# Graph attention kernel: edge lists and node inputs made in one stage, the rest of the lists beside the relation maxima, node maxima split during their gathers

## The reference

```python
h = relu(layernorm(x))
# first layer, for each relation r:
xr = (h @ W_rel[r]).reshape(N, H, D)
es, ed = einsum('nhd,hd->nh', xr, a_s[r]), einsum('nhd,hd->nh', xr, a_d[r])
logit = where(mask, leaky_relu(es[src] + ed[dst], 0.2), -1e30)
mx = segment_max(logit, dst)                    # one value per node, relation and head
p = exp(logit - mx[dst]) * mask
out = segment_sum(p / segment_sum(p, dst)[dst] * xr[src], dst)
# then gelu, W_cross, a softmax over relations; second layer: edge messages, segment_sum, two node products
```

## Time and profile before

| | us |
|---|---|
| median of 3 runs (5531.38 to 5540.8) | 5537.8 |
| profiled run | 5538.13 |
| its span | 5536.3 |
| lists, to the issue of node_inputs' first load | 239.2 |
| node_inputs, to the first gather of relation_maxima | 376.7 |
| relation_maxima, to the first operation of node_maxima | 1442.9 |
| node_maxima, to the first load of the attention | 1549.1 |

### The profile page before, as it was taken

How to read it: one execution, slowest core, us unless ns; L and a number is a source line. 1 busy time by engine, 2 the same in 40 slices (tenths; PEclk the granted TensorE clock), 3 DMA queues, 4 the chain that set the end, 5 groups by cost and what they waited for, 6 DMA issues and landing times. The chain is left out here.

```text
span 5536.3 us, 106419 instructions
## 1 busy us (share of the span) xinstructions
PE 3325.0 (60%) x16923; PEld 2273.1 (41%) x16924; DVE 3895.1 (70%) x11905; ACT 1426.1 (26%) x2966; POOL 3890.5 (70%) x3803
## 2 busy tenths in 40 slices
PE   0062222222156676244687877877887878778868
PEld 0031111111046665233354554545555545455537
DVE  4635555555578888887587777777777777777765
ACT  0130000000056666433322222222222222222222
POOL 3127777777679999721378888888878787888870
PEclk9685555555567778577899999999999999999989
DMA  2266666666256666412688888888888888888874
GB/s 57 60 182 194 193 196 192 194 194 193 81 126 153 154 155 154 150 42 76 183 183 182 179 180 179 180 179 179 178 177 182 177 180 177 180 179 182 177 144 141
DMA packets 725012, 891.72 MB, mean 161 GB/s; under 512 B 123241, under 2 KB 555465, under 8 KB 724710
## 3 DMA queue, kind: packets, MB, share of 16 engines
q0 software_dynamic: 217200, 396.10, 35.3%
q1 hardware_dynamic: 450742, 392.89, 24.9%
q10 hardware_dynamic: 56976, 101.87, 6.0%
HBM read 652.36 MB, written 238.06 MB: 161 GB/s over the span
## 5 line engine op out<-in xcount | busy, mean ns | idle before, releaser
L1529 POOL DMA_INDIRECT sums<-msg_bsum,k_sidx x831 | 1323.0, 1592 | 285.5 <-issue 241.7
L731 POOL DMA_INDIRECT max_xe<-rows,l_index x832 | 800.6, 962 | 426.6 <-issue 253.3
L1543 POOL DMA_INDIRECT msg_ga<-ab,k_bsrc x832 | 828.4, 996 | 368.7 <-issue 200.1
L1631 ACT ACTIVATE msg_low_ps<-msg_xs 128x512 f32<-128x512 f32 x928 | 558.0, 601 | 1986.8 <-DVE msg_xs L1600 1971.6
L1666 PEld LDWEIGHTS msg_both_ps<-msg_onehot,msg_hid 128*128 128x128 f32 x3712 | 552.0, 206 | 1216.7 <-DVE msg_bsum L1573 688.0
L1679 PE MATMUL msg_pre_ps<-msg_rw,msg_lt 128*128 128x512 f32 x1856 | 1030.0, 638 | 8.9 <-DMA msg_rw<-ab 8.9
L1666 PE MATMUL msg_both_ps<-msg_onehot,msg_hid 128*128 128x64 f32 x3712 | 616.4, 292 | 511.6 <-DVE msg_bsum L1573 500.4
L942 POOL TENSOR_SCALAR att_keyhot<-k_ramp,att_keys 128x128 f32<-128x128 f32 x1028 | 702.0, 703 | 56.1 <-ACT att_keys L1014 54.5
L1610 DVE TENSOR_TENSOR msg_hid<-msg_xs,msg_low_ps 128x512 f32<-128x512 f32 x928 | 634.5, 684 | 88.4 <-ACT msg_low_ps L1631 69.9
L1668 PE MATMUL msg_both_ps<-msg_hid,msg_same 128*128 128x256 f32 x1856 | 654.3, 437 | 0.0
L1599 DVE TENSOR_TENSOR msg_xs<-msg_pre_ps,msg_ga 128x256 f32<-128x256 f32 x928 | 388.9, 419 | 362.4 <-issue 157.4
(11 more groups left out here) (292 smaller groups left out, 5351.3 us busy)
## 6 DMA issues: line engine op xcount, KB each, us to landing
msg_rw<-ab SPq DMA_DIRECT2D x928, 128.0 KB
l_outside<-xe SPq DMA_DIRECT2D x1028, 72.0 KB, 2.7
xe<-max_xe SPq DMA_DIRECT2D x104, 576.0 KB, 3.0
max_src<-srcs ACTq DMA_DIRECT2D x104, 512.0 KB, 3.8
att_keyrow<-key ACTq DMA_DIRECT2D x257, 128.0 KB, 3.5
msg_lt<-in_efT SPq DMA_DIRECT2D x928, 32.0 KB
rows<-node_rows SPq DMA_DIRECT2D x50, 288.0 KB, 2.4
max_begin<-begin ACTq DMA_DIRECT2D x104, 128.0 KB, 2.5
```

The source lines that it names most:

```text
L731: pool.indirect_dma_start(xe[:, b, u, :], None, T.rows, bass.IndirectOffsetOnAxis(ap=K.index[:, k:k + 1], axis=0)).then_inc(s_xe[b], 16)
L1529: pool.indirect_dma_start(T.sums[k % 2], bass.IndirectOffsetOnAxis(ap=K.sidx[:, k:k + 1], axis=0), bsum[:, (k + 1) % SB, :], None, compute ...
L1543: pool.indirect_dma_start(ga[:, (k + 1) % RB, :], None, T.ab, bass.IndirectOffsetOnAxis(ap=K.bsrc[:, k:k + 1], axis=0)).then_inc(s_ga[k % ...
L1631: act.activation(low_ps[u % 2][:, :], xs[:, u % 2, :], ACT.Copy, scale=SLOPE1).then_inc(s_low, 1)
```

## The change

The stage `lists` goes. A phase `list` holds what outlives a stage (thresholds, gathered destinations, semaphores), and two stages share its work. `node_inputs` does the two counts of the windows at its start, the `rec` fields after x has been centred, and one count and one gather for each node tile inside the tile loop; six moves lie on ACT and PE before the loop, the last four of them between root and first normalisation. `relation_maxima` runs the rest on DVE in ticks 2 to 27 of its 104 (`beside`), with the first 32 ticks unrolled; the 17 gathers of steps, the keys, their moves and stores come after the group loop. `node_maxima` splits the `ed` term and then each half of the gathered maxima as soon as it is there, in separate buffers, with half of the copies on ACT.

```diff
-def lists(nc, K, T):
...
+def node_inputs(nc, K, T, S):
...
         @block.sync
         def _(sp):
+            sp.dma_start(first[:, :], T.first.to_broadcast([P, BLOCKS])).then_inc(s_first, 16)
             sp.dma_start(x[:, :, :], T.x.rearrange("(t p) c -> p t c", p=P)).then_inc(s_x, 16)
...
             sp.dma_start(att[:, :], T.att).then_inc(s_w, 16)
+            sp.dma_start(rec[:, :, :], T.rec[0:NB * P, :].rearrange("(j e) f -> j e f", e=GE)).then_inc(s_rec, 16)
...
+        @block.gpsimd
+        def _(pool):
...
+            for t in range(TILES):
+                c = t + 2
+                pool.wait_ge(S.s_made, INDEX + t + 1)
+                settle(pool, K)
+                pool.indirect_dma_start(S.dst[:, c, :], None, T.dst,
+                                        bass.IndirectOffsetOnAxis(ap=S.block_i[:, c:c + 1], axis=0)).then_inc(S.s_get, 16)
...
+            def count(t, b):
+                if past(t, 2):
+                    dve.wait_ge(s_cnt, t - 1)
+                dve.tensor_scalar(junk[:, b, :], first[:, :], S.thr[:, ds(t + 2, 1)], 0.0, ALU.is_lt, ALU.add,
+                                  accum_out=blocks[:, ds(t + 2, 1)]).then_inc(s_cnt, 1)
+
+            def number(t, b):
+                dve.wait_ge(s_cnt, t + 1)
+                dve.tensor_scalar(S.block_i[:, ds(t + 2, 1)], blocks[:, ds(t + 2, 1)], 1.0, 0.0,
+                                  ALU.subtract, ALU.max).then_inc(S.s_made, 1)
+
-            pipeline(dve, TILES, 2, [(0, evacuate), (1, rest)])
+            pipeline(dve, TILES, 2, [(0, evacuate), (0, count), (1, rest), (1, number)])
...
 def relation_maxima(nc, K, T, S):
...
+            pool.wait_ge(S.s_made, STEPLIST)
+            settle(pool, K)
+            for k in range(KKC):
+                pool.indirect_dma_start(kstep[:, k, :, :].rearrange("p f e -> p (f e)"), None, T.blk,
+                                        bass.IndirectOffsetOnAxis(ap=kplan.b[:, k:k + 1], axis=0)).then_inc(s_kget, 16)
+            for k in range(KC):
+                pool.indirect_dma_start(step[:, k, :, :].rearrange("p f e -> p (f e)"), None, T.blk,
+                                        bass.IndirectOffsetOnAxis(ap=plan.b[:, k:k + 1], axis=0)).then_inc(s_sget, 16)
...
+            def beside(t):
+                if t == 2:
+                    boundaries()
+                elif t == 4:
+                    offsets()
+                elif t == 5:
+                    kplan.pairs(dve, L, K, off[:, 0:KWINDOWS + 1], K.kgrid[:, :])
+                elif t == 8:
+                    plan.pairs(dve, L, K, off64[:, :], K.grid[:, :])
+                elif t == 10:
+                    schedule()
+                elif 12 <= t < 17:
+                    position(2 + (t - 12) * 10, 2 + (t - 11) * 10)
+                elif t == 17:
+                    lasts()
+                elif 18 <= t < 28:
+                    present((t - 18) * 5, (t - 17) * 5)
...
-            pipeline(dve, GROUPS, RG, [(2, scan), (1, separate), (2, firsts)])
+            ticks(dve, GROUPS, RG, 2, tick, AHEAD)
             dve.wait_ge(s_dup, 4 * GROUPS)
+            dve.wait_ge(s_kget, 16 * KKC)
...
 def node_maxima(nc, K, T, acc):
...
+            def split(g, values):
+                s, k = parts[g]
+                for i in range(TERMS):
+                    part = term[:, s, i, k, :]
+                    ins = dve.tensor_copy(part, values[:, k, :])
+                    if i < TERMS - 1:
+                        L.link(ins)
+                        L.link(dve.tensor_tensor(values[:, k, :], values[:, k, :], part, ALU.subtract))
+                    else:
+                        ins.then_inc(s_term, 1)
+                dve.wait_ge(s_term, g + 1)
+                for i in range(TERMS):
+                    for q in range(KQ // 2):
+                        for r in range(R):
+                            out, src = to_keys(s, i, k, q, r)
+                            dve.tensor_copy(out, src).then_inc(s_keyed, 1)
...
+            split(0, rest)
             L.mark(dve.memset(acc[:, :, :], 0.0))
-            dve.wait_ge(s_run, 16 * TILES)
...
+            for g in range(1, len(parts)):
+                s, k = parts[g]
+                n = k.stop - k.start
+                dve.wait_ge(s_run[g - 1], 16 * n)
```

More of the change, by code:

```diff
@@ L44 @@
 REC = 6
+THR = 2 + TILES
 PAD_DST = 1 << 20
@@ L303, in lists, with move_waits @@
+AT_NODES = INDEX + TILES
+DIAG, STEPLIST, KEY, LOC = range(AT_NODES + 1, AT_NODES + 5)
+def move_waits(pe, S, kind, row):
+    if kind == "row":
+        pe.wait_ge(row, 3)
+    elif kind == "index":
+        pe.wait_ge(S.s_made, INDEX)
+    elif kind == "key":
+        pe.wait_ge(S.s_made, KEY)
+    elif kind == "src":
+        pe.wait_ge(row, 16 * KC)
+    else:
+        pe.wait_ge(S.s_made, LOC)
+def node_inputs(nc, K, T, S):
+    with Phase(nc, "node") as ph:
         NG = NB // G
         GE = G * P
-        THR = 2 + TILES
@@ new lines, in node_inputs @@
+        tp_ps = [ph.ps(f"tp_ps{b}", [P, 4, P]) for b in range(2)]
+        s_first, s_rec, s_row, s_cnt = (ph.sem(n) for n in ("first", "rec", "row", "cnt"))
+        by_group = lambda t: t[:, :].rearrange("e (j u) -> e u j", u=G)
+        moves = []
+        for u in range(0, G, 4):
+            moves.append(("index", [index[:, v * P:(v + 1) * P] for v in range(u, u + 4)], by_group(K.index)[:, u:u + 4, :]))
+        for u in range(0, G, 4):
+            moves.append(("row", [fields[:, v, 0, :] for v in range(u, u + 4)], by_group(K.bsrc)[:, u:u + 4, :]))
@@ new lines, in node_inputs @@
+        for u in range(0, G, 4):
+            moves.append(("row", [fields[:, v, 2, :] for v in range(u, u + 4)], by_group(typT)[:, u:u + 4, :]))
+        NA = 2 * R + 2
+        RH = R * H
+        YS = 2 * RH
+        YW = YS + C + 2 * H
+        x = ph.sb("x", [P, TILES, C])
+        squares = ph.sb("squares", [P, TILES, C])
+        mean = ph.sb("mean", [P, TILES])
+        rstd = ph.sb("rstd", [P, TILES])
+        w_rel = ph.sb("w_rel", [P, R, C])
+        w_y = ph.sb("w_y", [P, YW])
+        w_t = ph.sb("w_t", [P, R + 1, C])
@@ new lines, in relation_maxima @@
+def relation_maxima(nc, K, T, S):
+    with Phase(nc, "max") as ph:
+        GROUPS = NB // G
+        RG = 4
+        RH = R * H
+        AHEAD = 32
+        xe = ph.sb("xe", [P, RG, G, XW])
+        begin = ph.sb("begin", [RH, 2, G * P])
+        m = ph.sb("m", [P, 2, G, RH])
+        run = ph.sb("run", [RH, 2, G * P])
+        runT = ph.sb("runT", [P, RG, G, RH])
+        srcf = ph.sb("srcf", [P, NB])
+        real = ph.sb("real", [P, 1])
+        src = ph.sb("src", [P, 2, G, P])
+        junk = ph.sb("junk", [P, G, P], BF16)
+        dup = ph.sb("dup", [P, G])
+        rowf = ph.sb("rowf", [P, G])
+        mT_ps = [ph.ps(f"mT_ps{b}", [RH, G * P]) for b in range(2)]
+        runT_ps = [ph.ps(f"runT_ps{b}", [P, G, RH]) for b in range(2)]
+        tile = ph.sb("tile", [P, P])
+        thr0 = ph.sb("thr0", [P, TILES])
@@ L804, in _ @@
             pipeline(act, GROUPS, RG, [(3, move_back), (1, begins), (1, sources)])
+            for g, (kind, ins, out) in enumerate(moves):
+                act.wait_ge(S.s_tp, MOVED + g + 1)
+                act.activation(out, tp_ps[g % 2][:, 0:len(ins), :], ACT.Copy).then_inc(S.s_cp, 1)
         @block.tensor
@@ L824, in back, with tick @@
                 last.then_inc(s_bk, 1)
-            pipeline(pe, GROUPS, RG, [(2, back), (1, transpose)])
+            def tick(t, h, has):
+                if isinstance(t, int) and t == 3:
+                    pe.wait_ge(S.s_made, DIAG)
+                    pe.matmul(off_ps, K.ones[:, :], flat(diag[:, :, :]), start=True, stop=True).then_inc(S.s_off, 1)
+                if has(2):
+                    back(t - 2, (h - 2) % RG)
+                if has(1):
+                    transpose(t - 1, (h - 1) % RG)
@@ L829, in node_maxima @@
+            ticks(pe, GROUPS, RG, 2, tick)
+            for g, (kind, ins, out) in enumerate(moves):
+                move_waits(pe, S, kind, s_sget)
+                if g >= 2:
+                    pe.wait_ge(S.s_cp, MOVED + g - 1)
+                for u, a in enumerate(ins):
+                    last = pe.transpose(tp_ps[g % 2][:, u, :], a, K.ident[:, :])
+                last.then_inc(S.s_tp, 1)
 def node_maxima(nc, K, T, acc):
     with Phase(nc, "top") as ph:
-        CH = 10
-        S2 = 2 * H
```

660 lines of the change are left out of this document (298 added, 362 removed).

## The result

The changed kernel takes 5338.75 us (median of four runs, 5335.70 to 5342.85) where the kernel before takes 5537.61: a ratio of 0.964, 95% interval 0.9627 to 0.9654. The forecast was 5348 with a range of 5315 to 5392, and the result lies in it. The profiled run took 5335.7, its span is 5333.8, against 5538.1 and 5536.3, so the two traces differ by 202.5 us in their spans.

| stretch | before | after | difference | forecast |
|---|---|---|---|---|
| to the first gather of the maxima | 376.7 | 165.7 | -211.0 | -204.3 |
| relation maxima | 1066.2 | 1093.8 | +27.7 | +29.9 |
| node maxima | 106.2 | 88.5 | -17.7 | -15.9 |
| all the rest | 3987.2 | 3985.7 | -1.5 | 0 |

What follows compares the result with a forecast made beforehand. No resource full in `lists`, a serial DVE-POOL-DVE chain; POOL's gathers set relation maxima. Terms -204.3 + 17.9 + 12 - 25.9 + 10 = -190.3 from 5538.1 gave 5348 us, range 5315 to 5392.

Steps and rivals of the forecast that it cites:

- Stage 1: Start to first gather of the maxima: 376.7 us falls to 172.4, a change of -204.3.
- The tile: Loop of node_inputs: 2.15 us a tile over the present 1.8, bounds 1.8 and 3.13, adding 17.5 us over 50 tiles.
- Rival A: Tile loop keeps its pace, the stores' turn absorbing the counts: -17.5, total 5330 us; chance 0.15.
- The tail: After the tile loop: four `outside` ops and the last gather's landing instead of a store's, +1.2 us.
- Stage 2: Relation maxima: DVE's added work hidden, 17 step gathers behind the 832 cost +17.9, slowed gathers +12 us.
- 0.69: Relation and node maxima: POOL loses 0.69 us per us of long two-input or wide DVE work; +12 and +10 us.
- Stage 3: Node maxima: split work overlapped with gathers ends the stage earlier, -25.9 us, less +10 for gathers slowed by DVE.
- rival C: Relation and node maxima: DVE and POOL exclude each other in full, +20 and +12 us, total 5381; chance 0.15.
- D: Tile loop: the added work comes serially, 3.13 us a tile, +49, total 5397 us; chance 0.12.
- E: Tile loop can't start until the counts are through: +56, total 5404 us; chance 0.03.
- F: Tile loop: gather and count hold each other up, stores queue behind; slower than before, 5538 us and more; chance 0.02.
- B: Relation and node maxima: long DVE operations cost POOL's gathers nothing, -22, total 5326 us; chance 0.08.

Runs made afterwards that it cites:

- second trace: The changed kernel itself run again, unedited, on chip 2 beside later variants: 5339.05 us, ratio 0.9641 to the kernel before.
- the pair of kernels with 2560 elements: Changed kernel plus one long unused DVE sum over 128 x 2560 elements per maxima group, on two operands or on one: 5630.2 and 5424.6 us.

## Why the prediction was right, and where its steps were off

**Stage 1, up to the tile loop: right.** Vectors landed at 23.67 (22.5 forecast), the sums began at 45.21 (45.5), the first normalisation at 55.96 (57.2). That `rec` queues behind x on SP cost about what was put down: DVE's cast of it began at 38.00. One thing was missed, and it was small: that cast took 2.81 us where it had taken 1.08, beside a cast of POOL's on the same data.

**The tile: inside its bounds, the reason wrong.** 2.15 was taken, between 1.8 and 3.13, and 1.914 came: 0.12 a tile were added and not 0.35. The step "it comes to 2.08, over the 1.8 at which two buffers of stores now turn" added the new work to a busy time. DVE's real sum is 1.73 a tile, and by the kernels with the counts first and the gathers behind even that isn't what counts: the loop with all the counts and no gathers is as quick as before. By the waits the bound was the stores all along. The step that failed is that the added engine work was priced, and POOL's gather, which was said not to be the bound, was only brought in by its bytes to confirm it. Rival A (the counts are absorbed in the wait for the stores) was right on its own ground; what it left out was the gather. Against the forecast this gave 50 x 0.236 = 11.8 us, some 10 by the second trace.

**The tail: 1.2 forecast, 6.3 more came.** This is the step that was most wrong for its size. From the last gather's end to the first act of the next stage it is 7.3 us, and to POOL's first gather there 7.9. With the counts first, where gathers had been done for 85 us, DVE's last operation ended at 206.15 and the next stage began at 206.65, 2.8 us after the issue of the last store. With all gathers behind the loop DVE was done at 149.65, the last gather ended at 211.47, and the next stage began 7.3 us later, at 218.74. So it is the gather that the border follows, and not DVE's work. Without the comparisons nothing was gained (7.9 us), and without POOL's wait for the landing 5.7 us were left. A border right behind a gather costs some 3 to 5 us more than one behind stores; POOL's wait for the landing is some 1.6 of it, and what the rest is stays open. -1.2 (the first normalisation) - 11.8 + 6.3 makes the -6.7 by which stage 1 beat its forecast; the 6.3 is what the other two leave.

**Stage 2: right in its sum.** The 832 gathers grew by 8.7 us (8 forecast), and from the last of them to the next stage it is 31.2 us in place of 12.2, +19.0 (17.9 and 4). That two-operand work holds a gather for 0.7 of its time is shown by the pair of kernels with 2560 elements. But of the 8.7 us it is only 4.4. Another 6.7 are spread evenly: the median gather takes 955 ns after and 947 before, 8 ns x 832, and all kernels with the changed lists have 955 or 958, on all chips. The short counts held gathers for some 2 us less than before, which makes up the sum; in the second trace of the changed kernel they held them for 1 us more, and the growth is 12.4 us. What lengthens each by 8 ns wasn't found. So this term came out right by luck, with half its cause wrong: 0.69 had been charged on 11 us, and DVE had some 9 us of two-operand work there. That the 68 us of DVE's work would be hidden was right (392.5 us of waits for a gather are left).

**Stage 3: right, two errors against each other.** The gathers took 5.5 us more (10 forecast): seven of them were held, three beside the first split and four beside that of the first half, and the 22.7 us of clearing beside them held none. The copies on ACT took 0.39 us and not 0.28; the stated bounds were 0.15 and 0.38 "each", the upper one being the row for 256 elements, and the row was right although the copy is of 200 elements in 32 partitions. It cost 2.6 us. What the prediction's own sums have wrong is small: the split adds up to 3.8 and not 3.9, and rival C to 5380 and not 5381.

**The rivals.** C, D, E and F fell by the total, and C by the 0.70 too: the lock is held in full, but the gather under way when DVE begins isn't stopped. B (long operations of DVE cost POOL nothing) fell by the pair of kernels. A was half right, as said. What no rival foresaw is the one effect that could have spoilt the forecast: the 308 instructions (526 with waits and accumulator reads) that DVE gained ahead of its loop of the messages. By luck they ended where nothing is fetched again; 12 more, and the changed kernel would have come out at 5429, with every step of the argument as it was.

## What to carry to other kernels

Before you add work to a loop, ask what ends its waits. This loop waited for its stores: DVE's counts beside it cost nothing, up to 0.96 busy, and a further gather on POOL cost 0.12 us a turn or more. Work laid beside POOL's gathers is sorted by its form: a long operation on two tensors stops POOL for 0.7 of its time, and a reduction or a comparison that counts into an accumulator does the same work free; a plain comparison with a scalar or a cast may stop it too, so look at the gather beside it. And when a stage that no edit touches changes length, compare the packets of fetched instructions and how many instructions stand ahead of the loop, waits included, before anything else.

## What the runs showed of the hardware that was not expected

- A loop of DVE instructions (260, or 315 with waits) is fetched again in each turn, or not, by where it stands: 12 instructions moved the kernel from 88 to 363 packets and by 89.8 us on chip 2; two kernels lost some 200 on chip 0.
- Chips differ in one stage above all: the gathers of the maxima are served at 156 GB/s on chip 0 and at 192 or 193 on the others, while the messages of the kernels with 83 to 89 packets take 2659 to 2669 us on chip 0 and 2647 to 2655 on the others.
- Which operations hold POOL's indirect gathers: sums, products and comparisons of two f32 tensors (the next gather ends 0.83 us behind a sum over 2560 elements), four comparisons of one f32 tensor with a scalar and casts from f32 to bf16 (0.11 and 0.12 us behind); hardly a reduction (2.81 us), and not counts with an accumulator (1.07 us) or a clearing (22.7 us).
- The undelayed gather takes 955 ns in one program and 947 in another, for the same rows.
- From the end of the last indirect gather of the lists to the next stage it is 7.3 to 7.9 us in eleven traces, and 5.7 in the one without POOL's wait for their landing, with nothing being moved for the last 3 to 5.
- DVE waits 4 to 5 us once a turn of the messages' loop, some 56 times, even where nothing is fetched again (4.56 in the row above). PE waits with it some 4 us. It lies outside this change and wasn't tried.
